# The square sum of a block's first pair, issued right behind that pair's output product

## The reference, cut to what matters

```python
zxbcdt = u @ in_w.T                                # input projection: z, xBC, dt
xBC = silu(conv_4_taps(xBC) + conv_b)              # xh, Bm, Cm
state = dA_t * state + dt_t * x_t (outer) B_t      # for each token t
y_t = state @ C_t
y = y + D * xh
y = y * silu(z)
y = y * rsqrt(mean(y * y) + EPS) * rms_w           # RMS norm over 1024 features
out = y @ out_w.T + res
```

## Time and profile before

| | us |
|---|---|
| median of 3 runs | 4570.46 (4567.15 to 4571.12) |
| the profiled execution, its own time | 4565.36 |
| its span, first to last instruction | 4563.6 |
| TensorE busy | 4091.3 (90%) |
| VectorE busy | 3353.1 (73%) |
| ScalarE busy | 2925.8 (64%) |
| GpSimd busy | 1979.6 (43%) |

### The profile page before, as it was taken

How to read it: one execution, slowest core, us unless ns; L and a number is a source line. 1 busy time by engine, 2 the same in 40 slices (tenths; PEclk the granted TensorE clock), 3 DMA queues, 4 the chain that set the end, 5 groups by cost and what they waited for, 6 DMA issues and landing times. The chain is left out here.

```text
span 4563.6 us, 100047 instructions
## 1 busy us (share of the span) xinstructions
PE 4091.3 (90%) x38872; PEld 3630.7 (80%) x38872; DVE 3353.1 (73%) x5217; ACT 2925.8 (64%) x4904; POOL 1979.6 (43%) x1572
## 2 busy tenths in 40 slices
PE   4499999999999999958999999999999998599999
PEld 1488888888888888848888888888888887477777
DVE  8588878787878787757877777777777776466664
ACT  4566666666666666746767666666666665565664
POOL 7244434343434344423434343434343444556664
PEclk6799999999999999979999999999999999799999
DMA  8300000000000000020000000000000000322220
GB/s 315 124 29 29 29 30 29 30 29 30 29 30 29 30 29 29 25 92 24 29 29 29 29 29 29 29 29 29 30 29 30 29 29 22 138 78 86 85 88 37
DMA packets 108673, 220.99 MB, mean 48 GB/s; under 512 B 10760, under 2 KB 11272, under 8 KB 107272
## 3 DMA queue, kind: packets, MB, share of 16 engines
q1 hardware_dynamic: 108176, 214.25, 13.3%
HBM read 146.97 MB, written 67.24 MB: 47 GB/s over the span
## 5 line engine op out<-in xcount | busy, mean ns | idle before, releaser
L502 PE MATMUL l_ring<-l_u_hi,l_wi_lo 128*128 128x256 f32 x4608 | 1324.9, 288 | 47.2 <-DVE l_u_lo L929 33.1
L502 PE MATMUL l_ring<-l_u_lo,l_wi_hi 128*128 128x256 f32 x4608 | 1302.4, 283 | 0.0
L502 PE MATMUL l_ring<-l_u_hi,l_wi_hi 128*128 128x256 f32 x4608 | 1301.2, 282 | 0.0
L502 PEld LDWEIGHTS l_ring<-l_u_hi,l_wi_lo 128*128 128x128 f32 x4608 | 880.6, 191 | 70.1 <-issue 33.8
L502 PEld LDWEIGHTS l_ring<-l_u_lo,l_wi_hi 128*128 128x128 f32 x4608 | 881.0, 191 | 12.5
L502 PEld LDWEIGHTS l_ring<-l_u_hi,l_wi_hi 128*128 128x128 f32 x4608 | 879.3, 191 | 0.0
L981 DVE SCALAR_TENSOR_TENSOR l_xc<-l_raw,l_prm,l_xc 128x256 f32<-128x256 f32 x1536 | 748.4, 531 | 110.3 <-ACT l_xc L757 92.1
L1166 POOL TENSOR_TENSOR l_g<-l_g 128x512 f32<-128x512 f32 (+2 forms) x384 | 340.4, 887 | 921.6 <-ACT l_g L818 901.6
L1137 POOL TENSOR_TENSOR l_rhs<-l_cum,l_small 32x1024 fp32r<-32x1024 f32 x256 | 485.3, 1896 | 260.9 <-PE l_wide L564 187.2
L502 PE MATMUL l_ring<-l_wo_hi,l_g_lo 128*128 128x512 f32 x1024 | 413.2, 403 | 23.1 <-DVE l_g_lo L1033 14.3
L502 PE MATMUL l_ring<-l_wo_hi,l_g_hi 128*128 128x512 f32 x1024 | 406.5, 397 | 0.0
(11 more groups left out here) (172 smaller groups left out, 8217.9 us busy)
## 6 DMA issues: line engine op xcount, KB each, us to landing
l_hn<-h_scratch SPq DMA_DIRECT2D x64, 512.0 KB, 4.0
l_res<-h_scratch SPq DMA_DIRECT2D x128, 256.0 KB, 3.8
h_scratch<-l_res SPq DMA_DIRECT2D x128, 256.0 KB, 2.1
m_rows<-in_x SPq DMA_DIRECT2D x16, 1024.0 KB, 9.5
h_scratch<-m_rows SPq DMA_DIRECT2D x16, 1024.0 KB, 7.2
f_x<-in_x SPq DMA_DIRECT2D x16, 1024.0 KB, 6.8
f_h<-h_scratch SPq DMA_DIRECT2D x16, 1024.0 KB, 8.5
out<-f_x SPq DMA_DIRECT2D x64, 256.0 KB, 2.0
```

The lines of the kernel that those rows point to most:

```text
L502: last = nc.tensor.matmul(out, a, c, start=(k == 0), stop=(k == n - 1))
```

## The change

The call of `square_sum` for pair 0 moves ahead of the odd chunk of pair 1. Nothing is added or removed.

```diff
                 out_product(b, s, 0, bank(s, USE_O[0]))
+                square_sum(b, s, 0)
                 states(b, s, 1, 1)
                 outputs(b, s, 1, 1)
-                square_sum(b, s, 0)
                 for n in (6, 7, 8):
                     proj(n)
```

## The result

| | us |
|---|---|
| before, median of 7 runs of this comparison | 4569.19 (4566.14 to 4571.56) |
| after, median of 7 runs | 4553.94 (4549.35 to 4555.11) |
| ratio, 95% interval | 0.9966 (0.9954 to 0.9977) |
| profiled execution of after, its own time | 4549.35 |
| its span | 4547.5 |

The change made the kernel faster by 0.34%, or 15.3 us. The two profiled spans differ by 4563.6 - 4547.5 = 16.1 us, which is about the difference of the medians, so the two traces can be compared.

The account below looks back on a forecast made before the run. TensorE without pause to `proj(8)`, then ScalarE, GpSimd and pair 1's line 605, set a block's length. Median 4570.46 us, less 6.7 work, plus 3.6 given back and 5.1 for new slow stretches, gave 4572.5; range 4558.8 to 4582.5.

Parts of the forecast that it names:

- The change on TensorE: At line 605 of pair 0: old place gives back 0.22 us, new place adds 0.12, so 0.10 saved per block.
- VectorE and GpSimd: `y_read`, gate, taps and line 1033 start 0.27 us earlier; the gap ahead of pair 1's product falls under 0.05.
- worth nothing in 62 blocks: The 0.27 us earlier VectorE work saves nothing there, because line 605 of pair 1 hangs on `proj(8)`.
- `proj(6)` and the cycle behind it start 0.10 us earlier: From `proj(6)` to the next block, everything on TensorE's cycle moves 0.10 us earlier per block, bounds 0.18 and 0.00.
- My sum of 6.7 us: Work saved over the kernel: 62 x 0.10 plus 2 x 0.27 us, the latter in each layer's last block.
- The clock, the term that I trusted least: A longer stand ahead of pair 1's line 605 brings three new slow stretches, 5.1 us, and 3.6 us given back.
- the turns aren't pinned: Claimed the reverse: the nine turns with a slow stretch keep their length near 228.6 us, giving back 3.6 us.
- Work saved, clock as it was: Rival: 6.7 us less work with the same nine slow stretches, 4563.8 us; chance 0.22.
- Nothing moves: Rival: the new place costs 0.22 us, what the old gave back; median stays at 4570.5 us; chance 0.11.
- slower by the clock: Rival: the longer stand gives every sequence one more slow stretch, 27.3 us less 6.7, so 4591 us; chance 0.14.
- A wait for the squares in front of the states: Rival: TensorE stands there beyond 4.54 us of room, each further microsecond costing 64 us; chance 1 in 100.
- My bound of 11.7 on the work: Upper bound in us on the work saved over the kernel, with 0.18 per block; the lower was 0.5.

Follow-up runs that it names:

- e3: The changed kernel plus one constant one-column filler matmul at the square sum's old place, ahead of the projections; 4586.77 us (one run).
- e4: The changed kernel with pair 0's square-sum matmul issued twice at its new place; 4588.52 us (one run).
- e2: The kernel before, with only VectorE's mean square of pair 0 moved behind the read of the odd chunk's outputs; 4552.81 us, ratio 0.9965.
- e5: The changed kernel, also with VectorE's mean square of pair 0 behind the read of the odd chunk's outputs; 4538.21 us, ratio 0.9936.
- e8: e2 plus four tiny VectorE memsets ahead of line 1033 of pair 1; 4552.18 us (one run).
- e10: The kernel before plus one one-column filler matmul ahead of pair 0's output product; 4571.44 us (one run).
- e1: Against the kernel before, pair 0's square sum stands between the odd chunk's states and its outputs; 4576.16 us, ratio 1.0016.
- e6: The changed kernel plus one one-column filler matmul ahead of pair 0's output product; 4585.98 us (one run).
- e9: The changed kernel plus two one-column filler matmuls ahead of pair 0's output product; 4622.44 us (one run).
- e7: The kernel before plus a small GpSimd addition ahead of pair 1's squares; 4620.25 us (one run).

## Why the prediction was wrong

**The change on TensorE.** Right. Line 605 has its input, the old place gives back 0.22 and the new place adds 0.12; the table gives 2.79 - 2.67 = 0.12 for the two together, where I had 0.10. e3 and e4 price the two places singly, at 0.23 and 0.24 beside a neighbour of the same kind.

**VectorE and GpSimd.** Right as far as it goes. Everything there moved by 0.26 to 0.27, and pair 1's product with it. The gap ahead of that product is 0.10 in the median block and not under 0.05, since `proj(8)` ended earlier than I had counted. I called a move of VectorE "worth nothing in 62 blocks". In work it is (e2: 0.6 us of 3346). In clock it isn't: e2 gained 17 us by the same lever in the other direction.

**The step that failed first: "`proj(6)` and the cycle behind it start 0.10 us earlier".** The start did, but the cycle behind did not stay as it was. The run of projections took 8.21 us in place of 8.30, so all behind it came 0.20 to 0.22 earlier. My sum of 6.7 us had no such term. 62 x 0.09 = 5.6 us were missing, and with the place at 0.12, 60 x 0.21 = 12.6 of the 15.0 us of work that the 60 blocks gave. The rest lies mainly in the 14 last blocks of a sequence, which average 58.43 before and 58.08 after. That the pace changed is shown; why it did is not.

**The clock, the term that I trusted least.** I had it take back 3.6 + 5.1 = 8.7 us, and it gave 0.8. Two steps failed. The first: the stand did not grow by 0.17, since proj(8) ended 0.09 to 0.10 earlier by the pace, and line 605 of pair 1 with it. It grew by 0.05 to 0.07, and seven short stretches lie inside the sequences instead of nine. The second: the turns aren't pinned. A turn of after with a short stretch took 228.15 (228.64 to 229.03 before), so the saved work came through. Their near-equal length before was no bound. Before, once they had begun in a layer, the short stretches came in one turn after the other, 228.69 us apart (1052.06 and 1280.75); after, mostly in every second turn (824.09 and 1278.10). That it became fewer and not more at a slightly longer stand, I can't explain, and it may be luck: each count is of one execution. I also left out the stretches at the ends of sequences, which cost 29.6 us before and 32.2 after. The direction that I gave, a longer stand costs clock, holds in the main over all the kernels, though not between before and after, and its price was far larger than I counted:

| kernel | e5 | e8 | e2 | e10 | before | after | e1 | e6 | e4 | e9 | e3 | e7 |
|---|---|---|---|---|---|---|---|---|---|---|---|---|
| stand | 0.29 | 0.57 | 0.62 | 0.71 | 0.81 | 0.86 | 0.86 | 0.96 | 0.96 | 0.96 | 1.17 | 1.40 |
| short stretches inside sequences | 0 | 0 | 0 | 0 | 9 | 7 | 7 | 13 | 16 | 19 | 16 | 28 |
| their cost | 0 | 0 | 0 | 0 | 15.4 | 11.9 | 11.9 | 22.2 | 27.3 | 32.4 | 27.3 | 47.8 |
| cost at the ends of sequences | 25.2 | 26.3 | 28.0 | 32.9 | 29.6 | 32.2 | 32.6 | 33.3 | 31.1 | 33.9 | 30.8 | 27.9 |
| clock, both | 25.2 | 26.3 | 28.0 | 32.9 | 45.0 | 44.2 | 44.5 | 55.5 | 58.4 | 66.3 | 58.1 | 75.7 |

The part inside the sequences goes with the stand. The part at their ends, where each trace has eleven stands of nearly 4 us ahead of line 540, does not.

Had the stand grown to 0.95 as I expected, the table says some 10 to 20 us more for the clock, where I had 8.7. Each point is one execution, the points at 0.96 differ by 11 us, and the nine runs of before beside e5 spread from 4557.98 to 4574.16, so it is a trend and no formula.

The Trainium skill, page "TensorE: Matmul & The Clock Gate", section "Terms", puts the penalty of time at half clock at half of that time. Two turns of the same work, one with a short stretch of 3.41 us more, differ by 228.15 - 226.01 = 2.14 us here, where half of it is 1.7. The rest lies in the longer stretch that each of the two turns has at the end of its sequence: TensorE is busy for 6.01 us of it in the one (from 882.10) and for 5.08 in the other (from 653.38), which is another 0.93 / 2 = 0.46. Before, 229.03 - 226.93 = 2.10 stands against 1.7 + (5.50 - 4.31) / 2 = 2.3. So the trace agrees within 0.2 us, if the time at half clock is counted where TensorE has work.

**The rivals.** "Work saved, clock as it was" is what happened, with twice the work. "Nothing moves" and "slower by the clock" did not, though e7, with 28 short stretches in place of nine, shows that the second one's mechanism is real. A wait for the squares in front of the states never came. My bound of 11.7 on the work was wrong in kind: it took both ends from the two places alone, and let everything behind them keep its duration.

## What to carry to other kernels

When TensorE is the bound and short slow stretches recur behind one stand, look at whether that stand can be made shorter by letting another one ahead of it grow. Here 0.98 us at pair 1 cost 45 us of clock as 0.17 + 0.81 and 25 us as 0.69 + 0.29, and the swap of two short VectorE instructions gave as much as the whole change. It is worth a try, and no rule: the 0.8 to 1.2 us ahead of line 564 brought no slow stretch here. Split the clock's cost by where the stretches lie first, since more than half of it was at the ends of sequences and stayed. And a sum made of one place's rows holds only if what follows keeps its pace, so compare the long runs of equal matmuls behind it before calling a range.

## What the hardware showed that I had not expected

**Two paces for the same run of matmuls.** The run of 72 matmuls of 256 columns, each with its weight load, at a granted clock of 1.00 and never idle, took 117.3 to 117.4 ns a matmul in four kernels and 118.6 to 118.7 in eight. That is the median block, one of the first three of a sequence. Single blocks leave their kernel's pace (two of the 24 of that kind in e6 ran at 117.3), and a sequence's last block took 117.5 to 120.6 ns in these traces. Neither the neighbours of the run, nor the count of short instructions, nor the start within the block accounts for it.

**The clock's price of a stand under one microsecond.** Inside the sequences TensorE fell to a granted clock of 0.50 for 3.41 us at a time, some 2 us behind stands of 0.81 us and more, and never in the four kernels with stands of 0.71 and less: the cost over 60 blocks was 0 there, 15.4 us at 0.81 and 47.8 at 1.40. The idle time at pair 1 was the same 0.96 to 0.98 in before, after, e1, e2, e4, e5, e6, e8, e9 and e10, so it is not its total alone that counts. Nor is it the length of one stand alone, since none followed the stand of 0.8 to 1.2 us ahead of line 564 in the same blocks. What tells the two stands apart was not tested. The Trainium skill says in the same page's section "What's actually happening" that the clock follows how busy TensorE has been recently. These runs agree with that, and add that the arrangement of the same idle time at pair 1 moved the number of short stretches between 0 (e5) and 19 (e9) in 60 blocks.
